# An attention and mixture-of-experts layer: an order worked out by a list scheduler, grouped diagonal tiles, sums of the softmax on other engines

## The chip, the cores and the metric

The kernel runs on one core of a Trainium2 chip. A core has TensorE (PE, matrix products into PSUM), VectorE (DVE), ScalarE (ACT), GpSimd (POOL) and SyncE (SP, which here only issues DMAs), each with an instruction stream of its own; they wait for each other on semaphores. The metric is the device time of the program in microseconds, from first to last instruction. Times are given in us unless marked otherwise.

## The reference

The input is x with 2 sequences of 1024 tokens and 128 features. Two sublayers follow each other, each between two layer normalisations:

```
x = x + layernorm(attention(layernorm(x)))
x = x + layernorm(moe(layernorm(x)))

attention: q = x @ wq                           8 heads of 128
           k, v from a latent of 32 per KV group, 2 groups, 4 heads to a group
           scores = q . k / sqrt(128), causal;  probs = softmax(scores);  y = (probs @ v) @ wo
moe:       32 experts of 64, in 4 groups; the best 2 groups (by the sum of their top 2), then the best 6 experts,
           weights = sigmoid scores of those, normalised, x 0.2
           out = sum of weight * (silu(x @ wg) * (x @ wu)) @ wd  + shared expert + 0.1 * anchor expert (of 16)
```

All products are wanted in about float32 precision. The kernel splits each float32 operand into a rounded high part and the low rest (`_hi`, `_lo`) and adds up three products, hi*hi, lo*hi and hi*lo (the helper `three`).

## The kernel before

**Tiling.** Tokens go in 4 chunks of 512 (two for each sequence). A block n is a chunk and a KV group: 8 blocks of 512 queries times 4 heads. A block of a sequence's first chunk has 4 key tiles of 128, one of the second chunk has 8. The latent of 32 is held three times over (96 rows: hi, hi, lo), so that one matmul of 96 rows gives a score in split precision.

**Two passes.** In the first pass (`p1`, L1046 with mask L1049) scores lie with queries on partitions: DVE takes the row maximum (L782), and ACT takes the exponential with a running sum for the softmax's denominator (L652; each sum is read by an extra accumulator read). The negative maximum, in three parts, becomes three more rows of q: POOL issues three DMAs for them (L587). In the second pass (`p2`, L1077 with mask L1079) scores lie with keys on partitions, ACT writes probabilities (L665), two heads at a time, and PE multiplies them with v (`pv`, L1095) into the bank `acc`.

**Mixture of experts.** An expert tile holds two experts; a chunk has 21 steps (16 expert tiles, 4 anchor tiles, 1 shared), 84 in all. A routed step has 10 matmuls of 512 columns: three for the gate (L974 to L976), three for the up product (the same lines), one that spreads the tokens' weights of this tile's experts over the partitions (L1138), three for the down product (L1150 to L1152). ACT does silu (L676) and the high part of h (L683), DVE two multiplications (L941, L942), POOL the low part (L620).

**Order.** `make_timeline` writes one list of events by hand rules (slots, lags, paces), and every engine walks through that list in order. One PSUM bank `misc` serves every small product, one `acc`, six serve scores. The queries of a block reach their place in 12 pieces by DMAs that SP issues (L521), from `q_hi` and `q_lo`. Weights of the attention are transposed on the chip at the start (L983, L987) and folded into each other (L993, L997).

Of the kernel before, what the change touches and what calls it, by code (L numbers as in the profile page):

```python
# [25 lines left out]
KROWS = QROWS + 3  # L50
# [8 lines left out]
MT = ET + LT + 1  # L59
WROWS = 3 * E + L  # L60
# [8 lines left out]
SBANKS = 6  # L69
KTBUF = 3  # L70
EXP_LAG = 0
DOWN_LAG = 3
AHEAD = 6
TAKE_LAG = 2
TOKEN_PACE = 4
TAIL = 8
SHORT = (1, 5)
SHORT_TAIL = 6
PROJ_LEFT = 4
PV_LAG = 2  # L80
PV_STEP = 3
YL_LAG = 1
QRING = 3


WSPLITS = range(0, MT, 3)
SPLIT_AT = (2, 3, 5)
MISC_KINDS = ("xT", "kproj", "vproj", "proj", "shift", "rb", "post_out", "post_T", "post_logits", "post_cwT", "fin_T")
ROUTE_STEPS = 9
PACE = 3  # L90
QUIET = ("load", "tables", "scale", "wsplit", "post_add", "fin_add")

TAKEN = ("xT", "kproj", "vproj", "proj", "shift", "rb", "post_T", "post_cwT")

TAKES = {"xn_mom": {"ln"}, "post_out": {"ln", "misc", "post"}, "post_logits": {"misc"}, "fin_T": {"ln", "misc"}, **{kind: {"misc"} for kind in TAKEN}}
GIVES = {"xT": {"ln"}, "post_nrm": {"misc"}, "post_T": {"ln"}, "post_logits": {"misc"}, "fin_nrm": {"misc"}, "fin_add": {"ln"}}


def make_timeline():

    line = []
    slots = 0
    held = set()
    agenda = []
# [12 lines left out]

    def may(ev):
        if ev[0] == "proj" and ("take", "xT", CPB * BLOCKS[ev[1]][0] + BLOCKS[ev[1]][1]) not in line:
            return False  # L120
        return not TAKES.get(ev[0], set()) & held

    def tick(limit=1, tensor=True):

        for c in list(agenda):
            while c[1] and c[0] <= slots and may(c[1][0][1]):
                ev = c[1][0][1]
                loud = ev[0] not in QUIET
                if loud and (limit == 0 or (ev[0] in MISC_KINDS and not tensor)):
# [1059 lines left out]
```

## Time and profile before

| | us |
|---|---|
| median of 3 runs | 528.27 (526.51 to 544.34) |
| span of the profiled execution | 536.1 |
| first matmul of a first pass | at 33.59 |
| last attention work, first of the experts | about 306.6 |
| last matmul of the experts | at 526.06 |

| engine | busy us | share of the span |
|---|---|---|
| PE | 467.0 | 87% |
| DVE | 352.8 | 66% |
| ACT | 306.9 | 57% |
| POOL | 200.7 | 37% |

Of the profiled execution the span is known, not its time by the other clock; it lies 1.5% above the median. PE's ends are modelled, so its busy share overstates its work: the distance from one start to the next is the better price of a matmul. The span has four stretches: a start in which little runs, the attention, the experts, and a tail of some 10 us after the last matmul.

### The profile page before, as it was taken

The numbers are of one execution on the slowest core, as the hardware profiler recorded it, in microseconds if no ns is written. First come the engines' busy times: TensorE is split into PE (matmuls) and PEld (weight loads), VectorE is DVE, ScalarE is ACT, GpSimd is POOL, SyncE is SP. The second block draws the span as 40 slices with busy tenths as digits, with TensorE's granted clock in tenths as the row PEclk, the third lists the DMA queues.
The fourth block names the chain that finished last, engine by engine and source line by source line (L and its number), as shares of the span: only waits on it lengthen the run. The fifth ranks groups of instructions, "written<-read, shape, count | busy, mean of one in ns | idle before, by whom it ended". The sixth has DMA issues, their size and how long they took to land.

```text
span 536.1 us, 7733 instructions
## 1 busy us (share of the span) xinstructions
PE 467.0 (87%) x2611; PEld 307.0 (57%) x2611; DVE 352.8 (66%) x937; ACT 306.9 (57%) x687; POOL 200.7 (37%) x216
## 2 busy tenths in 40 slices
PE   3657769889888999889989999999899989989992
PEld 2545445546455545446455667676677656667771
DVE  3345837575666479685692376989776698957662
ACT  2034758747786688898883456454345634445541
POOL 5000226051346001048011155455666456446553
PEclk9999999566996579999995899999999999999997
DMA  6263110300350500201000000000000000000000
GB/s 166 57 140 84 36 26 1 90 3 2 88 106 12 150 1 2 60 4 41 21 4 2 2 0 0 2 0 1 21 1 1 1 1 20 1 0 21 1 1 20
DMA packets 20472, 15.95 MB, mean 30 GB/s; under 512 B 8016, under 2 KB 15856, under 8 KB 20432
## 3 DMA queue, kind: packets, MB, share of 16 engines
q1 hardware_dynamic: 19664, 15.25, 11.6%
q8 instruction: 21, 0.34, 0.3%
q0 software_dynamic: 768, 0.20, 0.2%
q14 instruction: 19, 0.16, 0.1%
HBM read 6.32 MB, written 1.05 MB: 14 GB/s over the span
## 4 chain that ended last, share of the span: by engine, by line
PE 50%; DVE 26%; SPq 6%; POOL 5%; issue 5%; ACT 4%; DMA 1%; POOLq 0%; DVEq 0%; ACTq 0%
PE ps L1077 8%; PE acc L1095 7%; PE ps L1046 6%; DVE nmax_h L782 5%; PE ps L974 4%; DVE act_u L941 4%; SPq L521 4%; PE ps L976 4%; PE ps L975 4%; DVE h_sb L942 3%; ACT ps L652 2%; DVE normed L724 2%; POOL rstd L547 2%; PE acc L1150 2%; DVE stats L703 2%
## 5 line engine op out<-in xcount | busy, mean ns | idle before, releaser
L782 DVE TENSOR_REDUCE nmax_h<-ps 128x1 f32<-128x512 f32 (+3 forms) x192 | 98.0, 550 | 74.4 <-PE ps L1046 52.0
L652 ACT ACTIVATE ps<-ps,nmax_h 128x512 f32<-128x512 f32 (+3 forms) x192 | 106.1, 554 | 56.1 <-DVE nmax_h L782 55.5
L620 POOL TENSOR_TENSOR h_lo<-h_sb,h_hi 128x512 fp32r<-128x512 f32 (+1 forms) x84 | 108.7, 1298 | 78.4 <-ACT h_hi L683 78.4
L676 ACT ACTIVATE act_u<-ps 128x512 f32<-128x512 f32 (+1 forms) x84 | 50.2, 598 | 76.6 <-PE ps L976 76.4
L665 ACT ACTIVATE probs<-ps 128x1024 f32<-128x1024 f32 (+3 forms) x96 | 77.3, 815 | 19.8 <-PE ps L1079 12.5
L1077 PE MATMUL ps<-qst,kst 99*128 99x512 f32 (+3 forms) x192 | 80.5, 488 | 8.7 <-ACT ps L652 7.6
L1046 PE MATMUL ps<-kst,qst 96*128 96x512 f32 (+3 forms) x192 | 77.3, 486 | 10.7 <-DMA qst<-q_lo 9.8
L941 DVE TENSOR_TENSOR act_u<-act_u,ps 128x512 f32<-128x512 f32 x80 | 54.7, 684 | 43.7 <-PE ps L1138 25.8
L974 PE MATMUL ps<-xT_hi,w_hi 128*128 128x512 f32 x168 | 69.1, 412 | 8.4 <-DVE h_sb L942 7.3
L683 ACT ACTIVATE h_hi<-h_sb 128x512 fp32r<-128x512 f32 (+1 forms) x84 | 52.6, 626 | 30.8 <-DVE h_sb L942 29.5
L587 POOL DMA_DIRECT2D qst<-shift_rows x24 | 13.2, 553 | 140.8 <-DVE shift_rows L808 140.8
L976 PE MATMUL ps<-xT_hi,w_lo 128*128 128x512 f32 x168 | 65.6, 391 | 0.0
L975 PE MATMUL ps<-xT_lo,w_hi 128*128 128x512 f32 x168 | 65.6, 390 | 0.0
L1095 PE MATMUL acc<-probs,v_sb 128*32 128x256 f32 (+3 forms) x768 | 58.3, 386 | 3.5 <-ACT probs L665 2.0
L1077 PEld LDWEIGHTS ps<-qst,kst 99*128 99x128 f32 x192 | 43.0, 239 | 31.5 <-ACT ps L652 14.0
L1046 PEld LDWEIGHTS ps<-kst,qst 96*128 96x128 f32 x192 | 42.8, 251 | 30.3 <-DMA qst<-q_lo 10.2
L942 DVE TENSOR_TENSOR h_sb<-act_u,ps 128x512 f32<-128x512 f32 x80 | 55.0, 687 | 2.8
L1150 PE MATMUL acc<-h_hi,wd_hi 128*128 128x512 f32 (+1 forms) x84 | 47.9, 570 | 0.8 <-POOL h_lo L620 0.8
L974 PEld LDWEIGHTS ps<-xT_hi,w_hi 128*128 128x128 f32 x168 | 31.6, 188 | 23.2 <-DVE h_sb L942 16.2
L546 POOL TENSOR_SCALAR var_eps<-mv 128x4 f32<-128x4 f32 x16 | 3.7, 232 | 99.8 <-DVE mv L706 99.8
L652 ACT ACTIVATION_READ_ACCUMULATOR ps<-ps,nmax_h 128x1 f32 x192 | 38.6, 201 | 0.0
L976 PEld LDWEIGHTS ps<-xT_hi,w_lo 128*128 128x128 f32 x168 | 31.5, 188 | 6.9
(163 smaller groups left out, 715.0 us busy)
## 6 DMA issues: line engine op xcount, KB each, us to landing
qst<-q_hi SPq DMA_DIRECT2D x64, 64.0 KB, 2.0
qst<-q_lo SPq DMA_DIRECT2D x32, 64.0 KB, 2.0
x_sb<-in_attn_x SPq DMA_DIRECT2D x4, 256.0 KB, 5.7
kst<-k_hi SPq DMA_DIRECT2D x16, 64.0 KB, 2.0
result<-x_sb SPq DMA_DIRECT2D x4, 256.0 KB, 2.3
raw<-in_attn_wq SPq DMA_DIRECT2D x1, 512.0 KB, 3.8
raw<-in_attn_wo SPq DMA_DIRECT2D x1, 512.0 KB, 5.1
kst<-k_lo SPq DMA_DIRECT2D x8, 64.0 KB, 2.0
```

What stands on the lines that cost most here:

```text
L620: nc.gpsimd.tensor_tensor(h_lo[0:rows, k % 3, :], h_sb[0:rows, k % 2, :], h_hi[0:rows, k % 3, :].bitcast(F32), ALU.subtract).then_inc(h_lo ...
L652: nc.scalar.activation(scores, scores, ACT.Exp, bias=nmax_h[:, n % 2, i, j, h:h + 1], accum_out=sums_h[:, n % 2, i, j, h:h + 1]).then_inc( ...
L665: nc.scalar.activation(probs[:, k % KTBUF, 2 * p:2 * p + 2, off:CH], ps[:, BANK[ev]:BANK[ev] + 2, 0:CH - off], ACT.Exp).then_inc(slot_free, 1)
L782: nc.vector.tensor_reduce(nmax_h[:, n % 2, i, j, h:h + 1], ps[:, BANK[ev], 0:keys_of(ev)], AX.X, ALU.max, negate=True).then_inc(nmax_ready, 1)
L941: link(nc.vector.tensor_tensor(silu_u, silu_u, ps[:, bank + 1, :], ALU.mult))
L942: nc.vector.tensor_tensor(h_sb[:, k % 2, :], silu_u, ps[:, bank + 2, :], ALU.mult).then_inc(h_ready, 1)
L974: nc.tensor.matmul(dst, lhs[0], rhs[0], start=True, stop=False)
L975: nc.tensor.matmul(dst, lhs[0], rhs[1], start=False, stop=False)
L976: return nc.tensor.matmul(dst, lhs[1], rhs[0], start=False, stop=True)
L1046: last = nc.tensor.matmul(ps[:, BANK[ev], 0:keys], qst[0:QROWS, n % QRING, j, P * i:P * i + P], kst[0:QROWS, g, at:at + keys], start=True, ...
L1077: last = nc.tensor.matmul(ps[:, BANK[ev] + r, 0:CH - off], kst[0:KROWS, g, at:at + P], qst[0:KROWS, n % QRING, j, off:CH], start=True, sto ...
L1095: last = nc.tensor.matmul(acc[LAT * j:LAT * j + LAT, cols], v_sb[:, (T // P) * b + kt, LAT * g:LAT * g + LAT], probs[:, k % KTBUF, j, cols ...
```

## The change

Nearly every part of the program is written anew; what is computed stays the same.

- **Order.** `plan` gives every step an engine, a cost, a rank, the steps that it comes after and how many PSUM banks it takes until when; `Order.settle` places at each turn the step that can start first, the smaller rank where several can. Each engine walks its own list. All six banks serve scores, small products and experts alike; two more hold `acc` and `total`.
- **Start.** Small weights come from the host transposed and in one array; the folding (L1256, L1264) stays. Block 0's keys and queries go from PSUM straight to their place (`k0`, `q0`). PE runs 14 extra matmuls at the start (`warm`). SP issues 3 pieces per block for q rather than 12, and one for the rows of the maximum, now two rather than three.
- **First pass.** The exponentials on ACT and their sums are gone. The diagonal key tiles of several heads share a bank, so that 152 maxima remain of 192.
- **Second pass.** The four heads of a diagonal tile share a bank; 152 exponentials of at most 512 columns take the place of 96 of up to 1024. `pv` is 4 matmuls of up to 512 columns per key tile rather than 8 of half as many. The softmax's denominator comes from POOL, which adds the probabilities of two key tiles (`add`, 48 instructions), and PE, which multiplies the sums with ones into `total` (`ones`, 24 times 4 matmuls); DVE turns it into a reciprocal by two transposes (`recip`).
- **Normalisations** are applied by ACT rather than DVE.
- **Experts.** The weights of the experts are ordered so that one spread tile `cwb` serves 16 steps, made by two matmuls per chunk; a routed step has 9 matmuls. POOL multiplies silu's result with `cwb` (`mul`), DVE multiplies with the up product in PSUM (`h`) and takes the low part (`lo`). The routing of a chunk is cut into 24 DVE steps, placed among other work.
- **Tail.** The last normalisation runs in two halves of 256 tokens.

```diff
+def p2_steps(n):
+
+    out = []
+    for kt in range(kts(n)):
+        at = first_col(n, kt)
+        if on_diagonal(n, kt):
+            out.append(("p2", n, kt, 0, REP, at, P))
+            at += P
+        if at < CH:
+            w = CH // (CH - at)
+            w = 4 if w == 4 else 2 if w == 2 else 1
+            out += [("p2", n, kt, j, w, at, CH - at) for j in range(0, REP, w)]
+    return out
...
+        while any(ready.values()):
+            best = None
+            for engine, found in ready.items():
+                options = []
+                for ev in found:
+                    _, _, rank, after, width, _ = steps[ev]
+                    at = max([free[engine]] + [end[a] + HOP for a in after if steps[a][0] != engine])
+                    if width:
+                        at = max(at, min(banks_at(width))[0])
+                    options.append((at, rank, ev))
+                if options:
+                    soon = min(o[0] for o in options)
+                    pick = min((o for o in options if o[0] <= soon), key=lambda o: o[1])
+                    if best is None or pick[0] < best[0]:
+                        best = pick
...
+                        step("POOL", ("add", n, kt, half), 2 * (8 + cols * 252 // 1000), rank - 0.1, ("pv", n, kt - 1),
+                             *[e for e in exps if half in halves_of(e)])
+                    step("PE", ("ones", n, kt - 1), 10 + (CH - first_col(n, kt - 1)) * 17 // 100, rank - 0.2, ("add", n, kt, 0), ("add", n, kt, 1),
+                     kt == 1 and n >= 1 and ("recip", n - 1))
...
+            step("POOL", ("mul", k), 130, rank, ("silu", k), *([("cwb_copy", 0, m), ("cwb_copy", 1, m)] if t == 0 else []))
+            step("PE", ("u", k), 68, rank + 0.5, ("g", k), bank=1, until=("lo", k))
+            step("DVE", ("h", k), 69, rank - 1, ("mul", k), ("u", k))
...
                     for r, part in enumerate((q_hi, q_hi, q_lo)):
-                        for j in range(REP):
-                            sp.dma_start(qst[LAT * r:LAT * r + LAT, n % QRING, j, :].bitcast(F32), part[LAT * j:LAT * j + LAT, :].bitcast(F32)).then_inc(q_in[n % QRING], 16)
-                elif kind == "fin_add":
+                        sp.dma_start(qst[LAT * r:LAT * r + LAT, n % QRING, :, :].bitcast(F32), part[:].bitcast(F32)).then_inc(q_in[n % QRING], 16)
+                elif kind == "s_dma":
+                    n = ev[1]
+                    sp.wait_ge(copied, COPIED["shift_copy", n])
+                    if n >= QRING:
...
+                    nc.gpsimd.tensor_tensor(into, into, probs[:, k % KTBUF, js, cols], ALU.add).then_inc(added, 1)
...
-                    nc.gpsimd.tensor_tensor(h_lo[0:rows, k % 3, :], h_sb[0:rows, k % 2, :], h_hi[0:rows, k % 3, :].bitcast(F32), ALU.subtract).then_inc(h_lo_ready, 1)
...
+                    nc.gpsimd.tensor_tensor(silu[:, k % HRING, :], silu[:, k % HRING, :], cwb[:, m % 2, t // ET, :], ALU.mult).then_inc(scaled_ready, 1)
...
-                    nc.scalar.activation(scores, scores, ACT.Exp, bias=nmax_h[:, n % 2, i, j, h:h + 1],
-                                         accum_out=sums_h[:, n % 2, i, j, h:h + 1]).then_inc(slot_free, 1)
...
+                    link(nc.vector.transpose(rb[:], total[:]))
+                    link(nc.vector.reciprocal(inverse[:], rb[:].rearrange("p (q l) -> p q l", l=LAT)[:, :, 0]))
+                    nc.vector.transpose(rb[:].rearrange("p (q l) -> p q l", l=LAT), inverse[:].unsqueeze(2).to_broadcast([P, CH // LAT, LAT])).then_inc(recip_ready, 1)
...
-                        link(nc.vector.tensor_tensor(silu_u, silu_u, ps[:, bank + 1, :], ALU.mult))
-                        nc.vector.tensor_tensor(h_sb[:, k % 2, :], silu_u, ps[:, bank + 2, :], ALU.mult).then_inc(h_ready, 1)
...
+                    nc.vector.tensor_tensor(up, silu[0:rows, k % HRING, :], up, ALU.mult).then_inc(h_ready, 1)
+                elif kind == "lo":
+                    k = ev[1]
+                    rows = P if k in ROUTED else SI
+                    dve.wait_ge(h_hi_ready, H_HI["hi", k])
...
+                    s = bank(ev)[:, 0:w * cols].rearrange("p (w c) -> p w c", w=w)
+                    last = nc.tensor.matmul(s, kst[0:KROWS, g, at:at + P], qst[0:KROWS, n % QRING, j:j + w, first:first + cols], start=True, stop=not masked)
+                    if masked:
+                        last = nc.tensor.matmul(s, ident_bf[:], mask2[:].unsqueeze(1).to_broadcast([P, w, P]), start=False, stop=True)
...
+                elif kind == "ones":
+                    _, n, kt = ev
+                    cols = slice(first_col(n, kt), CH)
+                    pe.wait_ge(added, max(ADD["add", n, kt + 1, part] for part in range(2)))
+                    if kt == 0 and n >= 1:
+                        pe.wait_ge(recip_ready, n)
+                    for j in range(REP):
+                        last = nc.tensor.matmul(total[LAT * j:LAT * j + LAT, cols], ones[:], probs[:, KT[n, kt] % KTBUF, j, cols],
+                                                start=(kt == 0), stop=(kt == kts(n) - 2))
...
+                    nc.tensor.matmul(bank(ev), sel[:, part, :], cwT[:], start=True, stop=True).then_inc(misc_full, 1)
...
-                    if t < MT - 1:
-                        last = nc.tensor.matmul(ps[:, bank + 2, :], sel[:, t, :], cwT[:, m, :], start=True, stop=True)
```

The first place is PE's list in the experts, two steps of the steady state. Before, a step is three times three matmuls and the spreading matmul L1138:

```order
L974 MATMUL ps<-xT_hi,w_hi 128x512
L975 MATMUL ps<-xT_lo,w_hi 128x512
L976 MATMUL ps<-xT_hi,w_lo 128x512
L974 MATMUL ps<-xT_hi,w_hi 128x512
L975 MATMUL ps<-xT_lo,w_hi 128x512
L976 MATMUL ps<-xT_hi,w_lo 128x512
L1138 MATMUL ps<-cwT,sel 128x512
L1150 MATMUL acc<-h_hi,wd_hi 128x512
L1151 MATMUL acc<-h_lo,wd_hi 128x512
L1152 MATMUL acc<-h_hi,wd_lo 128x512
```

In the changed kernel it is:

```order
L1227 MATMUL ps<-xT_hi,w_hi 128x512
L1228 MATMUL ps<-xT_lo,w_hi 128x512
L1229 MATMUL ps<-xT_hi,w_lo 128x512
L1227 MATMUL ps<-xT_hi,w_hi 128x512
L1228 MATMUL ps<-xT_lo,w_hi 128x512
L1229 MATMUL ps<-xT_hi,w_lo 128x512
L1423 MATMUL acc<-h_hi,wd_hi 128x512
L1424 MATMUL acc<-h_lo,wd_hi 128x512
L1425 MATMUL acc<-h_hi,wd_lo 128x512
```

One matmul of ten has left the step; gate, up and down follow each other as before.

The second place is ACT's list in the middle of the attention. Before, exponentials of the first pass (L652, each followed by its accumulator read) stand between those of the second (L665):

```order
L652 ACTIVATE ps,sums_h<-ps,nmax_h 128x128 x2
L656 ACTIVATE scales<-scales 128x32
L665 ACTIVATE probs<-ps 128x2x384
L665 ACTIVATE probs<-ps 128x2x256
L627 ACTIVATE q_hi<-misc 128x512
L652 ACTIVATE ps,sums_h<-ps,nmax_h 128x256 x2
L665 ACTIVATE probs<-ps 128x2x256
L665 ACTIVATE probs<-ps 128x2x128
```

In the changed kernel ACT has exponentials of the second pass (L885), small copies, and four instructions for each normalisation of a chunk (L838):

```order
L885 ACTIVATE probs<-ps 128x512 x4
L838 ACTIVATE normed_p<-ps,offset,rstd 128x128 x4
L885 ACTIVATE probs<-ps 128x512 x6
L885 ACTIVATE probs<-ps 128x4x128
L885 ACTIVATE probs<-ps 128x384 x4
L885 ACTIVATE probs<-ps 128x4x128
L885 ACTIVATE probs<-ps 128x2x256
L838 ACTIVATE normed_p<-x_sb,offset,rstd 128x128 x4
L872 ACTIVATE shift_rows<-ps 8x512
```

The first pass has left ACT, and the normalisations have come to it.

The third place is POOL's list in the same part of the changed kernel (before, POOL has here the splitting of weights, the shift rows' DMAs and one addition per chunk). L747 is the addition of two key tiles' probabilities, L773 to L779 the splitting of weights, L710 to L713 the scale of a normalisation:

```order
L747 TENSOR_TENSOR probs<-probs 128x2x128 x2
L773 CAST w_hi<-raw 128x384
L774 TENSOR_TENSOR w_lo<-raw,w_hi 128x384
L773 CAST w_hi<-raw 128x256
L774 TENSOR_TENSOR w_lo<-raw,w_hi 128x256
L747 TENSOR_TENSOR probs<-probs 128x1024
L710 TENSOR_SCALAR neg_mean<-mv 128x4
L711 TENSOR_SCALAR var_eps<-mv 128x4
L712 TENSOR_TENSOR rstd<-var_eps,half_power 128x4
L713 TENSOR_TENSOR offset<-neg_mean,rstd 128x4
```

A normalisation's scale and a PE `ones` product now stand behind an addition of two tiles on the same engine.

## Rows read from the trace of the kernel before

**Rows 1.** Busy time by stretch: start:end, length, busy us of each engine (instructions), granted clock, DMA.
```profile
0.00:33.60 33.60, 16.26 (x73) 13.09 (x73) 11.90 (x38) 4.69 (x6) 8.30 (x18) 1.00 0.44 115
...
82.60:195.30 112.70, 101.80 (x612) 59.97 (x608) 71.69 (x183) 81.38 (x210) 35.56 (x49) 0.73 0.22 54
195.30:280.60 85.30, 78.81 (x666) 44.80 (x662) 63.93 (x229) 73.84 (x185) 20.86 (x31) 1.00 0.09 21
...
306.60:527.00 220.40, 207.66 (x924) 148.82 (x916) 165.77 (x371) 107.62 (x181) 122.45 (x101) 1.00 0.02 4
```

**Rows 2.** Chain of waits up to 35 us: start, us, what; a piece that SP issues is SPq.
```profile
5.40 1.04 POOL rstd L547
...
22.29 0.51 SPq L521
...
29.18 0.59 SPq L521
```

**Rows 3.** Timeline of PE around the first matmul of a first pass: start, us, engine, line, tiles.
```profile
33.16 0.63 PE L976 MATMUL misc<-xT_hi,wkv_lo 128*128 128x512 f32 x1
33.59 0.31 PE L1046 MATMUL ps<-kst,qst 96*128 96x128 f32 x1
```

**Rows 4.** Groups of instructions, 195.3 to 280.6, by form: busy us, mean ns | idle before, releaser.
```profile
L1077 PE MATMUL ps<-qst,kst 99*128 99x512 f32 x50 | 18.9, 455 | 2.8 <-ACT ps L652 2.5
L1046 PE MATMUL ps<-kst,qst 96*128 96x512 f32 x32 | 13.5, 468 | 0.6 <-ACT probs L665 0.6
L1095 PE MATMUL acc<-probs,v_sb 128*32 128x256 f32 x204 | 16.6, 395 | 1.2 <-ACT probs L665 0.9 <-issue 0.2
```

**Rows 5.** Timeline of PE at 255, the clock granted in full.
```profile
254.90 0.73 PE L1077 MATMUL ps<-qst,kst 99*128 99x512 f32 x2
255.57 0.64 PE L1095 MATMUL acc<-probs,v_sb 128*32 128x256 f32 x8
256.14 0.73 PE L1077 MATMUL ps<-qst,kst 99*128 99x512 f32 x2
```

**Rows 6.** Groups of instructions over the whole span, as in rows 4.
```profile
L652 ACT ACTIVATE ps<-ps,nmax_h 128x512 f32<-128x512 f32 (+3 forms) x192 | 106.1, 554 | 56.1 <-DVE nmax_h L782 55.5
L652 ACT ACTIVATION_READ_ACCUMULATOR ps<-ps,nmax_h 128x1 f32 x192 | 38.6, 201 | 0.0
L782 DVE TENSOR_REDUCE nmax_h<-ps 128x1 f32<-128x512 f32 (+3 forms) x192 | 98.0, 550 | 74.4 <-PE ps L1046 52.0 <-PE ps L1049 21.7
```

**Rows 7.** ACT's exponentials of the second pass, widest and narrowest form.
```profile
L665 ACT ACTIVATE probs<-ps 128x1024 f32<-128x1024 f32 x48 | 48.9, 1029 | 7.1 <-PE ps L1079 3.8 <-PE ps L1077 3.1
...
L665 ACT ACTIVATE probs<-ps 128x256 f32<-128x256 f32 x16 | 6.1, 384 | 4.8 <-PE ps L1079 3.0 <-PE acc L1095 1.7
```

**Rows 8.** The same as rows 6 over the whole span, the lines of an expert step, and a normalisation.
```profile
L941 DVE TENSOR_TENSOR act_u<-act_u,ps 128x512 f32<-128x512 f32 x80 | 54.7, 684 | 43.7 <-PE ps L1138 25.8 <-POOL h_lo L620 10.1 <-ACT act_u L676 7.3
...
L620 POOL TENSOR_TENSOR h_lo<-h_sb,h_hi 128x512 fp32r<-128x512 f32 x80 | 103.6, 1299 | 72.8 <-ACT h_hi L683 72.8
L676 ACT ACTIVATE act_u<-ps 128x512 f32<-128x512 f32 (+1 forms) x84 | 50.2, 598 | 76.6 <-PE ps L976 76.4
L724 DVE TENSOR_SCALAR normed<-x_sb,mv,rstd 128x128 f32<-128x128 f32 x32 | 11.0, 405 | 4.3 <-POOL rstd L547 4.3
```

**Rows 9.** Timeline of PE in the experts at 483, one step from L1138 to L1138.
```profile
483.03 0.39 PE L1138 MATMUL ps<-cwT,sel 112*128 112x512 bf16 x1
...
485.32 0.39 PE L1138 MATMUL ps<-cwT,sel 112*128 112x512 bf16 x1
```

**Rows 10.** DVE's L876 (both inputs in SBUF): 195.3 to 280.6, then 306.6 to 527.
```profile
L876 DVE TENSOR_TENSOR ties<-ties,lower 128x64 f32<-128x64 f32 x1 | 0.2, 224 | 0.0
...
L876 DVE TENSOR_TENSOR ties<-ties,lower 128x64 f32<-128x64 f32 x2 | 2.5, 1271 | 0.1
```

**Rows 11.** Timeline from the last matmul, all engines: start, us, engine, line [idle before].
```profile
526.06 0.39 PE L1152 MATMUL acc<-h_hi,wd_lo 64*128 64x512 f32 x1
...
533.41 0.37 SPq L525 DMA_DIRECT2D result<-x_sb  x1
```

More of the change, by code:

```diff
@@ new lines, with kts, first_col, pack @@
+ROUTE_STEPS = len(ROUTE_COST)
+ROUTED = {k: n for n, k in enumerate(k for k in range(NU) if k % MT != SHARED)}
+def kts(n):
+    return TPC * (BLOCKS[n][1] + 1)
+def first_col(n, kt):
+    return P * max(0, kt - TPC * BLOCKS[n][1])
+def pack(cols):
+    return 4 if cols == P else 2 if cols == 2 * P else 1
+def p1_steps(n):
+    c = BLOCKS[n][1]
+    out = []
+    for i in range(TPC) if n else reversed(range(TPC)):
+        own = pack(P * (i + 1))
+        out += [("p1", n, i, j, 0, 1) for j in range(REP) if c]
+        out += [("p1", n, i, j, c, own) for j in range(0, REP, own)]
+    return out
@@ new lines, with count @@
+KT_AT = [(n, kt) for n in range(NB) for kt in range(kts(n))]
+KT = {at: k for k, at in enumerate(KT_AT)}
+PLACED, PLAN = plan()
+BANK, BEFORE = PLACED.bank, PLACED.before
+def count(engine, *kinds):
+    return {ev: k + 1 for k, ev in enumerate(e for e in PLAN[engine] if e[0] in kinds)}
+MISC = count("PE", "xT", "k0", "q0", "kproj", "vproj", "proj", "am", "am2", "shift", "post_out", "post_T", "post_logits", "post_cwT", "cwb", "fin_T")
+SCORES = count("PE", "p1", "p2")
+PV = count("PE", "pv")
+ONES = count("PE", "ones")
@@ new lines @@
+G = count("PE", "g")
+U = count("PE", "u")
+DOWN = count("PE", "down")
+HI = count("ACT", "xT_hi", "a3_hi", "a_hi", "k0_hi", "q0_hi", "k_hi", "q_hi", "post_T_hi")
+NORMED = count("ACT", "xn_nrm", "post_nrm", "post_nrm2", "fin_nrm")
+COPIED = count("ACT", "m_copy", "v_copy", "shift_copy", "cwT_copy", "cwb_copy", "post_tanh", "fin_copy")
+EXP = count("ACT", "exp")
+SILU = count("ACT", "silu")
+H_HI = count("ACT", "hi")
+LO = count("DVE", "xT_lo", "a3_lo", "a_lo", "k0_lo", "q0_lo", "k_lo", "q_lo", "post_T_lo")
@@ new lines @@
+MAX = count("DVE", "max")
+MOM = count("DVE", "xn_mom", "post_mom", "post_mom2", "fin_mom")
+H = count("DVE", "h")
+H_LO = count("DVE", "lo")
+RSTD = count("POOL", "xn_rstd", "post_rstd", "post_rstd2", "fin_rstd")
+ADD = count("POOL", "add")
+MUL = count("POOL", "mul")
+WSPLIT = count("POOL", "wsplit")
+LN = {ev: k for k, ev in enumerate(MOM)}
+MOM_OF = {"xn_rstd": "xn_mom", "post_rstd": "post_mom", "post_rstd2": "post_mom2", "fin_rstd": "fin_mom",
+          "xn_nrm": "xn_mom", "post_nrm": "post_mom", "post_nrm2": "post_mom2", "fin_nrm": "fin_mom"}
@@ new lines, in _ @@
+                    for kc in range(CPB * b, CPB * b + c + 1):
+                        if kc:
+                            pe.wait_ge(k_in[kc], 16 * 3)
+                        else:
+                            pe.wait_ge(lo_ready, LO["k0_lo", g])
+                    pe.wait_ge(masks, 3)
+                    bank_turn(ev)
+                    at = T * b + CH * h
+                    keys = p1_cols(ev)
+                    s = bank(ev)[:, 0:w * keys].rearrange("p (w k) -> p w k", w=w)
+                    for r in range(w):
+                        last = nc.tensor.matmul(s[:, r, :], qst[0:QROWS, n % QRING, j + r, P * i:P * i + P], kst[0:QROWS, g, at:at + keys],
+                                                start=(r == 0), stop=(h < c))
```

1700 lines of the change are left out of this document (953 added, 747 removed).

## The prediction, on record before the changed kernel ran

> **What bounds the kernel now.** I read the table of stretches first [rows 1]. Up to 33.6 us PE is busy less than half the time and no score has been computed. From 82.6 to 306.6 lies most of the attention, with a mean granted clock of 0.73 up to 195.3: PE runs at 1.2 GHz for more than half of that stretch. From there to 280.6 it is 1.00, which is 2.4 GHz. From 306.6 to 527 lie the experts, at 1.00 throughout. PE looks busy nearly everywhere, but its ends are modelled, so I price a matmul by the distance between starts.
>
> In the full-clock stretch of the attention (85.3 us) I count what PE did [rows 4, 5]. Two score matmuls of 512 columns take 255.57 - 254.90 = 0.67 us, eight rows of `pv` of 256 columns 0.57 us. So 82 score matmuls of 512 are 27.5 us and 204 rows of `pv` 14.5 us; with the narrower ones and the small products, which I estimate at 26 us, 68 of 85.3 us, or 0.80, were work. What holds PE back is ACT, busy for 73.84 of 85.3 us (0.87) [rows 1]. It does the exponential of both passes, and 201 ns of accumulator reading for each of 192 in the first; DVE's maxima in turn wait 52.0 us for PE, and ACT 55.5 us for them [rows 6].
>
> In the experts a step takes 485.32 - 483.03 = 2.29 us for ten matmuls, 0.229 each [rows 9]. Eighty such steps and four shared ones of nine matmuls are 183 + 8 = 191 us of 220.4.
>
> **The start.** SP's twelve pieces of q take 22.29 to 29.77 (12 rows of about 0.6) [rows 2], and the first score follows at 33.59 [rows 3]. The change writes block 0's q and k straight to their place, and PE no longer transposes the small weights. What is left is a chain: scale of the normalisation to 6.44 [rows 2], then by estimate 0.8 to apply it, 0.7 to transpose, 1.3 for the two halves, 1.3 for three matmuls at half clock (0.43 each, as from 33.16 to 33.59 [rows 3]), 1.3 again for halves; the folded weights a3, which need wq, may end later. That is 12 at the least and 22 if the weights' chain sets the end. I take 15.5: 18 us less. `warm` runs while PE has nothing else, at no cost, unless it goes on past the first transposes, which is inside these bounds.
>
> **Attention.** *ACT* loses the first pass, 106.1 + 38.6 us [rows 6]. The second pass is 152 instructions rather than 96 over the same 73,728 columns: 1024 columns take 1029 ns and 256 take 384 [rows 7], so 0.84 ns per column and 0.17 us beside them, 62 + 26 = 88 us. With normalisations (some ten in the attention, four pieces each of about 0.4 us, as DVE's 405 ns [rows 8]) and copies ACT has some 125 us, and no longer bounds anything.
>
> *PE*, at full clock. A score matmul of 512 costs 0.229 in a run of its kind [rows 9] and 0.335 where kinds alternate [rows 5]; I take 0.28. First pass: 96 of these and 96 narrower ones at 0.2 to 0.33 with their masks (estimates in proportion), 52 us. Second pass: 152 groups at about 0.29, 45 us. `pv`: 24 key tiles of 512 columns at 1.0 (twice 0.57 less a start [rows 5]) and 24 narrower at 0.25 to 0.8, 37 us. New `ones`: 16 at 1.0 and 8 at 0.57, 20 us. Projections, transposes and small products 27 us, and 10 us more for changes of kind: 191 us. Before, the same count without `ones` and with dearer `pv` gives about the same, so PE gains nothing in work; it gains that nobody holds it up.
>
> *DVE* keeps 152 maxima of 97 us in place of 98.0, for the same columns [rows 6], loses the normalisations (11.0 us for those out of SBUF [rows 8], about as much for those out of PSUM) and gains 8 `recip` (three instructions, two of them of 512 columns, each some 0.69 [rows 8]: 13 us). With the low parts, moments and two chunks' routing it has 165 us.
>
> *POOL* gets 48 additions of 32,768 columns in all. By L620, 1299 ns for 512 columns [rows 8], that is 83 us; with what it has there already, 35.6 + 20.9 us [rows 1], about 140 us. A `ones` product waits for an addition, and a probability buffer comes free with it (four buffers): with a pair of full key tiles POOL needs 5.2 us, PE in the second pass alone 5.4 us.
>
> *SP* issues three q pieces per block rather than twelve, and the maximum's rows in one DMA, which POOL issued in three. On SP that one stands behind up to six pieces of 0.6 us [rows 2] and the loads of weights, 2 to 4 us; the first pass of the next block covers it, and where that is used up PE waits so long, once per block, 8 times at the worst (inside the end of 0.80 below).
>
> So the fullest engine after PE has 165 of some 230 us. The old kernel reached 0.80 with ACT at 0.87. I take 0.87 for PE, with ends 0.80 and 0.95: 191 / 0.87 = 220 us (201 to 239). To that I add 10 us for 1.2 GHz: in the first 20 us of the attention PE still waits for tokens and weights. Attention ends at 15.5 + 220 + 10 = 245 us, before at 306.6.
>
> **Experts.** Nine matmuls at 0.229 make a step of 2.06 us: 80 steps 165 us, four shared ones 5.5 (two products, six matmuls), transposes and logits of the chunks some 10: 180 us. DVE has two instructions of 0.684 us in a step, 1.37 as before, POOL 1.30 as before, ACT two instructions of some 0.6 [rows 8]. The spreading matmul, for which DVE waited 25.8 us [rows 8], is gone from the step; what stands in its place is POOL's multiplication between silu and `h`, 1.3 us longer in latency, covered by three buffers rather than two. Before, 29 us of 220.4 were lost, mostly where routing held DVE; routing is now cut into 24 pieces. I take 16 us lost: 196 (188 to 215).
>
> **Tail.** From the last matmul at 526.06 to the store's issue at 533.41 are 7.35 us [rows 11]; in halves the middle steps are half as long and lie beside each other: 4.3, 3 us less.
>
> **Sum.** 536.1 - 18 (start) - 43.6 (306.6 - 33.6 = 273 of attention becomes 229.5) - 24.4 (experts) - 3 = 447 us. The profiled execution lies 1.5% above the median of 528.27, so 447 x 528.27 / 536.1 = 441 us.
>
> **Where a rule speaks against it.** The row: L876, with both inputs in SBUF, took 224 ns where POOL was mostly idle and 1271 ns in the experts, where POOL runs 1299 ns instructions [rows 8, 10]; L941, with one input in PSUM, took 684 ns beside the same POOL. The Trainium skill says in "SBUF — State Buffer", section "Who interferes with whom", that a DVE instruction with two SBUF inputs and a GpSimd instruction lock each other out of a shared port for a whole instruction. The trace agrees, with 1271 against 224 ns. By that rule alone the longer additions would make the second rival below likelier.
>
> **The rivals.**
>
> *(a) PE alone bounds (0.15).* No wait matters and the clock stays up after the start: 15 + 201 + 3 + 190 and 10 behind, 419 on the span and 413. For: no other engine has over 0.72 of the attention. Against: lists fixed in advance by costs that don't meet the chip's durations leave waits on four engines.
>
> *(b) POOL and DVE lock each other out (0.17).* DVE has some 100 instructions in the attention with SBUF inputs alone (rows of maxima, reciprocals, two routings). Where POOL is busy 0.6 of the time with instructions of 1.3 to 2.6 us, each may wait up to 1 to 2.6 us: 40 to 90 us on DVE's 165, which makes DVE the bound, at 205 to 255 of 230, and some 15 us more in the experts. Then the attention takes 20 to 25 us more and the time is 475 to 485. It decides once DVE's stretch passes some 50 us.
>
> *(c) Slower: the clock stays at 1.2 GHz (0.03).* For: 0.43 us per matmul at 33.2 [rows 3] after a start in which PE was half idle, and a mean of 0.73 from 82.6 to 195.3, where waits for ACT and DVE also left it unevenly fed [rows 1, 6]. If the new waits keep PE at 1.2 GHz through the attention, its 191 us become 382: 15 + 382 / 0.95 + 196 + 10 = 623, slower than before. It decides once some 90 us of the attention's full-clock work run at the half clock beyond what I count, which alone costs as much again and brings 447 to 536 on the span. Against: the experts stay at 1.00 with 29 us lost.
>
> *(d) The lists don't fit (0.04).* The changed list keeps engines waiting for each other as much as the old one (0.80 and worse), the experts gain only the tenth matmul: 15.5 + 250 + 205 + 7, 478 on the span and 471.
>
> **The numbers.** The forecast, 441, has 0.61, with its own range of 420 to 465. With (a) below it and (b), (d) above, 405 to 484 holds 8 in 10. A change of 2% is 10.6 us, about what a measurement can tell: 518 and 539 are far from all cases but (c). Faster 0.95, same 0.02, slower 0.03.
>
> **What would show it.** The first score near 15 us; ACT under 0.6 busy in the attention; the attention's end near 245; steps of 2.06 us between the down products; DVE's reciprocal and routing rows at a multiple of their 200 ns would speak for (b), a granted clock of 0.5 beyond 40 us for (c). I am wrong in the main step if PE's starts lie no denser in the attention than 0.80 of its work.

## The result: 438.65 us, the forecast 441, by two misses that nearly cancel

The changed kernel takes 438.65 us (median of 4 runs, 436.96 to 440.96). The ratio to the kernel before is 0.8337, with a 95% interval of 0.8276 to 0.8397. That is inside the range, and close to the 441 us that was forecast. A second measurement beside later runs gave 438.91 (436.47 to 442.81, 6 runs).

The kernel before takes 522 to 551 us, longer where less clock was granted (a mean of 0.94 at 522 us, 0.87 at 551): the ratio is from its shorter, undisturbed runs (spans of 520 to 527 us), while its trace is of a longer one (536.1), so that some 10 of the 98.5 us between the two traces are that run's. Below, a part of the kernel is compared by its stretch in a trace. I cut the span at events that both kernels have: the first score, the first gate product of the experts, the last down product.

| | before | changed | forecast |
|---|---|---|---|
| start, to the first score | 33.6 | 16.9 | 15.5 |
| attention, to the first gate product | 273.2 | 213.8 | 229.5 |
| experts, to the last down product | 219.2 | 199.4 | 195 |
| tail | 10.1 | 7.5 | 7 |
| span | 536.1 | 437.6 | 447 |

The forecast's 196 us for the experts were counted from 306.6 to 527, 1.2 us more than this cut; hence 195.

### The profile after

The first score, the answer to [rows 3], and the tail, the answer to [rows 11], from the timelines of PE and of SP:

```profile
16.93 0.40 PE L1317 MATMUL ps<-kst,qst 96*128 96x512 f32 x1
...
430.10 0.38 PE L1425 MATMUL acc<-h_hi,wd_lo 64*128 64x512 f32 x1
```
```profile
434.35 1.39 SPq L672 DMA_DIRECT2D result<-x_sb  x2
```

The first half's store is issued 4.25 us after the last matmul, where it was 7.35 for the whole. The stretches of the changed kernel, one answer to [rows 1], with columns as there:

```profile
0.00:16.90 16.90, 13.85 (x66) 12.06 (x67) 10.75 (x36) 6.12 (x12) 8.82 (x30) 0.90 0.45 132
16.90:230.70 213.80, 197.29 (x1250) 105.55 (x1248) 157.92 (x388) 108.66 (x219) 121.29 (x121) 0.94 0.28 52
230.70:430.50 199.80, 190.01 (x842) 146.56 (x838) 155.46 (x363) 113.04 (x209) 121.30 (x111) 0.99 0.02 5
430.50:437.60 7.10, 1.11 (x4) 0.71 (x4) 3.05 (x16) 1.91 (x6) 1.49 (x2) 0.51 0.12 37
```

For the attention of the kernel before, the two stretches that [rows 1] did not show in this cut:

```profile
33.60:82.60 49.00, 36.84 (x146) 24.46 (x144) 28.57 (x76) 28.89 (x92) 8.14 (x10) 1.00 0.28 61
82.60:306.80 224.20, 205.80 (x1490) 120.31 (x1486) 144.12 (x442) 165.58 (x409) 59.23 (x85) 0.82 0.15 35
```

The 1.00 of the first of these is not a grant but the lack of a record. The distances of its masked scores, at 45, 60, 74 and 81 us, are those of 1.2 GHz; at 45 us 0.67 us from one score to the next:

```profile
45.06 0.78 PE L1046 MATMUL ps<-kst,qst 96*128 96x512 f32 x1
45.64 0.33 PE L1049 MATMUL ps<-mask,ident_bf 128*128 128x128 bf16 x1
45.73 0.78 PE L1046 MATMUL ps<-kst,qst 96*128 96x512 f32 x1
```

The same pair in the changed kernel, at 2.4 GHz, takes 0.36 us:

```profile
17.88 0.48 PE L1317 MATMUL ps<-kst,qst 96*128 96x512 f32 x1
18.20 0.23 PE L1320 MATMUL ps<-mask,ident_bf 128*128 128x128 bf16 x1
18.24 0.48 PE L1317 MATMUL ps<-kst,qst 96*128 96x512 f32 x1
```

From these rows the gain of the attention can be taken apart. Before, PE was busy for 36.84 + 205.80 = 242.6 us, and ran at 1.2 GHz for the first 49.0 us and 78.5 of recorded grants (a mean of 0.82 over 224.2 us is as much, within its rounding), 127.5 us in all. Changed, it is busy for 197.3 us, with 27.3 us at 1.2 GHz. PE's busy time within those stretches is the number behind the length; before, from 82.6 us on:

```profile
96.30:116.80 20.50, 19.35 (x96) 12.19 (x92) 12.31 (x36) 11.86 (x32) 3.96 (x7) 0.50 0.21 51
120.20:130.40 10.20, 9.71 (x51) 6.60 (x52) 4.66 (x10) 7.77 (x25) 3.01 (x5) 0.50 0.01 2
164.60:195.30 30.70, 30.70 (x151) 16.81 (x149) 16.10 (x48) 21.58 (x53) 5.25 (x7) 0.50 0.27 70
280.60:297.70 17.10, 17.10 (x102) 9.40 (x99) 5.22 (x17) 7.09 (x11) 1.54 (x3) 0.50 0.01 2
```

and changed:

```profile
27.90:34.70 6.80, 4.89 (x17) 4.10 (x18) 3.27 (x8) 1.76 (x5) 2.28 (x4) 0.50 0.52 189
58.60:65.40 6.80, 6.75 (x25) 3.58 (x25) 4.76 (x10) 1.77 (x5) 4.39 (x6) 0.50 0.83 119
120.10:130.30 10.20, 9.30 (x24) 4.36 (x24) 7.30 (x13) 4.67 (x8) 2.35 (x4) 0.50 0.00 0
222.50:225.90 3.40, 3.40 (x15) 2.13 (x15) 3.23 (x23) 1.12 (x3) 0.00 (x0) 0.50 0.00 0
```

So PE was busy at 1.2 GHz for 36.8 + 76.9 = 113.7 us before and for 24.3 now. Of that time 0.46 is lost by the pair of scores above (0.67 us for 0.36), or half by the ratio of the clocks (1.2 to 2.4 GHz): 53 to 57 us before, 11 to 12 now. By this estimate **41 to 45 of the 59.4 us came with the clock**. PE's idle time fell from 30.6 to 16.5 us, 14 us more. What is left, 186 to 190 us of full-clock work before and 185 to 186 now, is nearly the same: the sums by `ones` cost about what the longer products of `pv` save. The 191 us of the forecast were 3% too many.

The busy share of PE hardly shows any of this (0.89 before, 0.92 now), and in two of the old stretches at 1.2 GHz PE was busy throughout. In which part the 10 us named above fall, no trace tells. The one other trace of the same attention code (the kernel before without the spreading matmul, below) has an attention of 274.5 us with 129.6 at 1.2 GHz, a second one of the changed kernel 212.6 with 23.9.

The costliest waits of PE in the changed kernel (us in all, times, the longest):

```profile
PE ps L1317 <- DMA qst<-q_lo: 6.1, 2, 3.8
PE ps L1388 <- DVE weights L1140: 4.6, 2, 3.1
PE acc L1423 <- DVE h_lo L1159: 4.0, 6, 1.2
PE ps L1372 <- ACT silu L913: 3.2, 1, 3.2
PE total L1362 <- POOL probs L747: 3.2, 3, 1.8
```

L1423 and one of the two L1388 (1.5 us) lie among the experts' steps, L1372 at the passage to them, the others before it. The step is what was priced: in this piece of timeline, from a first product to that of the next step, nine matmuls take 382.69 - 380.62 = 2.07 us, against 2.29 for ten in [rows 9].

```profile
380.62 0.39 PE L1227 MATMUL ps<-xT_hi,w_hi 128*128 128x512 f32 x1
...
382.00 0.40 PE L1423 MATMUL acc<-h_hi,wd_hi 128*128 128x512 f32 x1
382.24 0.39 PE L1424 MATMUL acc<-h_lo,wd_hi 128*128 128x512 f32 x1
382.46 0.40 PE L1425 MATMUL acc<-h_hi,wd_lo 128*128 128x512 f32 x1
382.69 0.39 PE L1227 MATMUL ps<-xT_hi,w_hi 128*128 128x512 f32 x1
```

### The profile page after: what moved, and what is told of

Its sections match the earlier page's. It is cut to its first block, busy times and chain, and to the rows that moved or that the text cites. A ratio compares the mean times of both kernels' runs of the same rounds, so it can differ in the third digit from the quotient of the medians.

```text
span 437.6 us, 6989 instructions
## 1 busy us (share of the span) xinstructions
PE 402.3 (92%) x2156; PEld 264.9 (61%) x2156; DVE 327.2 (75%) x800; ACT 229.7 (53%) x445; POOL 252.9 (58%) x263
## 3 DMA queue, kind: packets, MB, share of 16 engines
q1 hardware_dynamic: 9584, 13.49, 15.5%
## 4 chain that ended last, share of the span: by engine, by line
PE 65%; DVE 21%; issue 4%; DMA 3%; ACT 3%; POOL 2%; SPq 1%; POOLq 0%; DVEq 0%; ACTq 0%
PE ps L1317 8%; PE ps L1338 8%; PE ps L1227 7%; PE ps L1229 7%; PE ps L1228 7%; PE acc L1352 7%; PE acc L1423 4%; DMA qst<-q_lo 3%; PE total L1362 3%; PE acc L1425 3%; PE acc L1424 3%; DVE ps L1154 3%; DVE nmax_h L1039 2%; PE ps L1372 2%; DVE h_lo L1159 2%
## 5 line engine op out<-in xcount | busy, mean ns | idle before, releaser
L787 POOL TENSOR_TENSOR silu<-silu,cwb 128x512 f32<-128x512 f32 x80 | 103.2, 1296 | 64.0 <-ACT silu L913 63.2
L885 ACT ACTIVATE probs<-ps 128x512 f32<-128x512 f32 (+1 forms) x152 | 80.1, 578 | 72.6 <-PE ps L1338 38.1
L747 POOL TENSOR_TENSOR probs<-probs 128x768 f32<-128x768 f32 (+2 forms) x48 | 78.1, 1645 | 59.9 <-ACT probs L885 37.1
L1159 DVE TENSOR_TENSOR h_lo<-ps,h_hi 128x512 fp32r<-128x512 f32 (+1 forms) x84 | 57.2, 685 | 22.0 <-ACT h_hi L923 21.5
L1154 DVE TENSOR_TENSOR ps<-silu,ps 128x512 f32<-128x512 f32 (+1 forms) x84 | 57.8, 691 | 16.1 <-POOL silu L787 12.9
L923 ACT ACTIVATE h_hi<-ps 128x512 fp32r<-128x512 f32 (+1 forms) x84 | 50.1, 598 | 32.4 <-DVE ps L1154 28.0
L913 ACT ACTIVATE silu<-ps 128x512 f32<-128x512 f32 x80 | 47.6, 599 | 36.4 <-PE ps L1229 30.9
L1338 PE MATMUL ps<-qst,kst 98*128 98x512 f32 (+1 forms) x152 | 64.1, 462 | 1.5 <-ACT probs L885 0.5
L1317 PEld LDWEIGHTS ps<-kst,qst 96*128 96x128 f32 x192 | 36.3, 204 | 30.7 <-issue 20.5
L1352 PE MATMUL acc<-probs,v_sb 128*32 128x512 f32 (+3 forms) x384 | 41.2, 513 | 0.3 <-issue 0.2
L1338 PEld LDWEIGHTS ps<-qst,kst 98*128 98x128 f32 x152 | 29.8, 204 | 16.5 <-issue 14.9
L1423 PE MATMUL acc<-h_hi,wd_hi 128*128 128x512 f32 (+1 forms) x84 | 35.5, 423 | 4.2 <-DVE h_lo L1159 4.0
L1424 PE MATMUL acc<-h_lo,wd_hi 128*128 128x512 f32 (+1 forms) x84 | 33.2, 395 | 0.0
```

What stands on the lines that cost most here:

```text
L747: nc.gpsimd.tensor_tensor(into, into, probs[:, k % KTBUF, js, cols], ALU.add).then_inc(added, 1)
L787: nc.gpsimd.tensor_tensor(silu[:, k % HRING, :], silu[:, k % HRING, :], cwb[:, m % 2, t // ET, :], ALU.mult).then_inc(scaled_ready, 1)
L885: nc.scalar.activation(probs[:, k % KTBUF, j:j + w, at:at + cols], bank(full)[:, 0:w * cols].rearrange("p (w c) -> p w c", w=w), ACT.Exp). ...
L1154: nc.vector.tensor_tensor(up, silu[0:rows, k % HRING, :], up, ALU.mult).then_inc(h_ready, 1)
L1159: nc.vector.tensor_tensor(h_lo[0:rows, k % HRING, :], bank(("u", k))[0:rows], h_hi[0:rows, k % HRING, :].bitcast(F32), ALU.subtract).then_ ...
L1317: last = nc.tensor.matmul(s[:, r, :], qst[0:QROWS, n % QRING, j + r, P * i:P * i + P], kst[0:QROWS, g, at:at + keys], start=(r == 0), stop ...
```

## Experiments

Two theories of the attention were tried against each other, that ACT held it and that the new order, with or without the clock, made the gain; then what sets the experts' pace, what the additions on POOL cost, and two small edits that the waits above point to.

### The first-pass exponential put back

```diff
+            step("ACT", once, wide * (42 + cols * 80 // 1000), rank, peak, x and ("once", *steps[x - 1][1:]))
...
-                        pe.wait_ge(max_ready, MAX["max", *user[1:]])
+                        pe.wait_ge(once_done, ONCE["once", *user[1:]])
...
+                        last = nc.scalar.activation(scores, scores, ACT.Exp, bias=nmax_h[:, n % 2, i, j + r, h:h + 1],
+                                                    accum_out=sums_h[:, n % 2, i, j + r, h:h + 1])
```

> The changed kernel with one part undone: ACT again takes the exponential of the first pass, with its running sum and accumulator read (192 instructions in the plan, each first-pass bank is held until it is done; the sums are not used further). Theory A, ACT held the attention before and its relief is what shortened it: ACT gets some 145 us more (192 of about 0.55 and 0.2) on the 116 it has between 17 and 246, 261 us of busy time in a stretch of 229.5, so the attention must grow to 275 to 300 us and the time from 438.65 to 485 to 510, with ACT at 0.85 to 0.95 busy there. Rival B, the new order and PE's longer products shortened it and ACT does not matter: under 450.

492.67 us (490.51 to 496.54): 54 us more, as theory A had it. The lists are worked out anew with these steps in them. The attention's stretch, and the two groups that came back:

```profile
14.80:281.50 266.70, 219.68 (x1249) 109.88 (x1247) 153.28 (x365) 212.77 (x607) 121.65 (x124) 0.88 0.23 42
```
```profile
L885 ACT ACTIVATE ps<-ps,nmax_h 128x512 f32<-128x512 f32 (+3 forms) x192 | 108.9, 573 | 35.5 <-DVE nmax_h L1056 34.9
...
L885 ACT ACTIVATION_READ_ACCUMULATOR ps<-ps,nmax_h 128x1 f32 x192 | 43.4, 226 | 0.0
```

It takes 266.7 us, near the 273.2 of before, with 64.9 us at 1.2 GHz and 47 us of idle PE. ACT is busy for 0.80 of it. On the expectation's own cut, to the last out product (14.75 to 296.4), the attention is 281.7 us, inside its 275 to 300, with ACT at 0.78 and not 0.85 to 0.95. So with the new order and everything else in place, this one part is worth most of the gain of the attention.

### The same part taken out of the kernel before

```diff
-                    nc.scalar.activation(scores, scores, ACT.Exp, bias=nmax_h[:, n % 2, i, j, h:h + 1],
-                                         accum_out=sums_h[:, n % 2, i, j, h:h + 1]).then_inc(slot_free, 1)
+                    nc.scalar.activation(sums_h[:, n % 2, i, j, h:h + 1], scores[:, 0:1], ACT.Exp, bias=nmax_h[:, n % 2, i, j, h:h + 1]).then_inc(slot_free, 1)
```

> The kernel before, its order untouched, with ACT's first-pass exponential cut to one column and without the running sum (so the softmax's denominators are left out of the computation). ACT loses some 100 us (192 times about 0.33, and the accumulator reads 38.6) of 232 in the attention. Theory A, ACT held PE at 0.80 there: the attention shortens by 35 to 50 us, ratio 0.91 to 0.935. Rival B, the old order's hand rules, the waits for DMAs and the 1.2 GHz stretches held it: under 10 us, ratio over 0.98.

523.98 us (510.45 to 541.15), the kernel before beside it 528.55 (527.21 to 545.41). Theory A falls for the old kernel: in the trace its attention still takes 261.8 us, 11 less, and lowest run against lowest is 16.8 us. That is more than rival B's 10 and half of theory A's least.

```profile
33.50:295.30 261.80, 236.49 (x1632) 140.89 (x1630) 172.52 (x518) 129.00 (x308) 67.54 (x94) 0.86 0.18 41
```

ACT's busy time in the attention fell from 194.5 (not the 232 of the expectation) to 129 us, but PE's busy time from 242.6 only to 236.5. The time at 1.2 GHz hardly moved: 71.7 us of recorded grants from 78.5. ACT waited for DVE's maxima instead, 98.5 us in place of the 55.5 of [rows 6]:

```profile
ACT sums_h L652 <- DVE nmax_h L781: 98.5, 121, 6.4
```

### And the maxima thinned as well

```diff
-                    nc.vector.tensor_reduce(nmax_h[:, n % 2, i, j, h:h + 1], ps[:, BANK[ev], 0:keys_of(ev)],
+                    nc.vector.tensor_reduce(nmax_h[:, n % 2, i, j, h:h + 1], ps[:, BANK[ev], 0:64],
```

> The kernel before with the first-pass exponential of one column (as in the run before it) and the maxima taken over 64 columns rather than up to 512, so that neither ACT nor DVE can hold the first pass (the softmax is left out of the reference's form: maxima and denominators are of a part). Relieving ACT alone took the attention from 273 to 262 us only. Theory C, DVE's maxima were next in line behind ACT: the attention falls to 210 to 235 us. Rival D, the order and the 1.2 GHz stretches that come with it (49 us from 33.6 to 82.6, and 72 after that) hold PE: it stays at 245 us or more, with 90 us or more at 1.2 GHz.

491.47 us (489.09 to 493.68), the kernel before beside it 537.24 (522.87 to 548.0); lowest against lowest is 33.8 us, and by the traces the attention is 47.9 us shorter.

```profile
33.40:258.70 225.30, 207.80 (x1632) 128.21 (x1630) 113.88 (x518) 126.02 (x308) 66.93 (x94) 0.94 0.21 48
```

Theory C holds. The old order can do the attention in 225.3 us, if neither DVE nor ACT holds a first-pass bank long. So the order alone was not the limit: in the kernel before a bank went from PE to DVE's maximum, from there to ACT's exponential, and only then back. PE had the same matmuls in that run; it was at 1.2 GHz for 27.3 us of recorded grants, in place of 78.5 (and in the first 30 us of the attention, of which there is no record, in place of 49).

The changed kernel reaches 213.8 us with the maxima at full width (DVE busy for 157.9 us of them and all else). So it takes both: ACT's step gone from the first pass, and lists in which PE does not wait for DVE's maxima though they are as long as before. Which rule of the list does the second (banks for all purposes, their release by the maximum, or the packing of 192 maxima into 152) was not taken apart and stays open.

### A tenth matmul in the experts' step

```diff
+                    if k in ROUTED:
+                        nc.tensor.matmul(total[:], sel[:, t // ET, :], spread[:], start=True, stop=True)
```

> The changed kernel with a tenth matmul of 512 columns in each of the 80 routed expert steps (a product of the selection matrix with a constant, into the bank of the sums, which nothing reads). Theory A, PE's matmuls alone set the experts' pace now: 80 x 0.229 = 18.3 us more, 457. Rival B, waits between the engines or DVE set it: less than 5 us more, under 444.

457.61 us (454.15 to 460.08), 19 us more, 457 expected by theory A. The experts' stretch grew by 17.5 us, from 199.8 to 217.3:

```profile
227.80:445.10 217.30, 206.17 (x922) 150.65 (x918) 157.51 (x363) 113.30 (x210) 120.93 (x111) 0.99 0.02 4
```

The tenth matmul is paid nearly in full (18.3 us by its price): the experts are bound by PE.

### The tenth matmul taken out of the kernel before

```diff
-                    if t < MT - 1:
+                    if k < 2:
                         last = nc.tensor.matmul(ps[:, bank + 2, :], sel[:, t, :], cwT[:, m, :], start=True, stop=True)
```

> The kernel before with the spreading matmul only in the first two expert steps (the later steps multiply with what stands in the bank, so the weights of the experts are left out of the computation). Theory A, PE's ten matmuls set the step also before: 78 x 0.229 = 18 us less, ratio 0.966. Rival B, DVE's second multiplication and POOL's low part set it (DVE waited 25.8 us for this matmul, but PE also waited 7.3 us for DVE): under 6 us less, ratio over 0.99.

530.9 us (518.6 to 531.75) against 528.55, which the scatter doesn't tell apart; lowest against lowest is 8.6 us. By the traces the experts went from 219.2 to 210.7 us, 8.5 and not 18, so both theories are half right. PE's wait for DVE's multiplications grew as the matmul went, from 7.3 us in 14 waits to

```profile
PE ps L974 <- DVE h_sb L942: 15.9, 20, 2.3
```

In the old kernel half of the matmul's price lay on the path; without it PE came sooner to a wait for the two multiplications that stand in series on DVE. In the changed kernel a tenth matmul is paid nearly in full, and between gate and down product the same work is spread over POOL, DVE and ACT; that the spreading makes the difference was not tried by itself.

### No additions on POOL

```diff
-                if kt % 2:
-                    for half in range(2):
-                        step("POOL", ("add", n, kt, half), 2 * (8 + cols * 252 // 1000), rank - 0.1, ("pv", n, kt - 1),
-                             *[e for e in exps if half in halves_of(e)])
...
+                step("PE", ("ones", n, kt), 10 + cols * 17 // 100, rank - 0.2, *exps, kt == 0 and n >= 1 and ("recip", n - 1))
```

> The changed kernel without POOL's additions: PE multiplies every key tile with ones, not every second one. POOL loses 78 us; PE gains 8 products of 512 columns at 0.97, 8 of 384 at about 0.78 and 8 of 128 at about 0.36, 17 us. Theory A, PE bounds the attention: 12 to 17 us slower, 450 to 456. Rival B, POOL's long instructions on the port that DVE shares with it (or POOL itself) hold the attention: no slower, 430 to 440; in both the rows of DVE with SBUF inputs alone return to their short times.

441.21 us (440.39 to 442.5), 2.6 us more, between the theories. By the expectation PE has 17 us more to do, and the attention grows by 5.3 us only:

```profile
14.80:233.90 219.10, 206.19 (x1458) 111.08 (x1456) 143.24 (x355) 109.75 (x223) 47.98 (x79) 0.95 0.27 51
```

The rest is seen: PE is idle for 12.9 us in place of 16.5, and at 1.2 GHz for 20.5 in place of 27.3 (busy for 15.7 of them in place of 24.3, some 4 us less lost), together 8 us; and the full-clock work, counted as above, grew by 13 us, not 17. The start and the experts are 2 us shorter each. Rows of DVE with inputs in SBUF alone are short again, as both theories said. In the changed kernel, and then without the additions, the routing of the chunk that falls into the attention:

```profile
L1132 DVE TENSOR_SCALAR wsum<-wsum 128x4 f32<-128x4 f32 x1 | 1.7, 1699 | 0.0
L1128 DVE TENSOR_SCALAR dist<-dist 128x64 f32<-128x64 f32 x1 | 1.5, 1512 | 0.0
```
```profile
L1120 DVE TENSOR_SCALAR dist<-dist 128x64 f32<-128x64 f32 x1 | 0.2, 184 | 0.0
L1124 DVE TENSOR_SCALAR wsum<-wsum 128x4 f32<-128x4 f32 x1 | 0.2, 171 | 0.0
```

The Trainium skill's rule on the port that DVE and GpSimd share ("SBUF — State Buffer", section "Who interferes with whom"), which counts `tensor_scalar` among the operations that can contend for it, agrees with this, 1512 ns against 184. But what the stretched rows take beyond their short times comes to some 12 us of DVE's time in the attention, not 40 to 90, and DVE had room for it.

### The start without its extra matmuls

```diff
-WARM = 14
+WARM = 0
...
-    step("PE", ("warm",), 560, 0)
+    step("PE", ("warm",), 0, 0)
```

> The changed kernel without the 14 matmuls at the start. Theory A: they fill time in which PE has nothing to do, and PE's clock is granted in full earlier for them; without them the matmuls from 7.5 to 17 us run longer at 1.2 GHz and the first score comes 1 to 3 us later: 440 to 442. Rival B: they only delay the first weight products, which start at 7.55 right behind them: the first score comes up to 2 us sooner, 436 to 438.

439.3 us (438.93 to 439.46), no difference to be told from 438.65. In the trace the first score came at 19.0, later than in all nine traces that have the extra matmuls (14.8 to 18.2). The 16 weight products behind them show why; with the extra matmuls, and then without:

```profile
7.55 1.87 PE L1256 MATMUL ps<-small_w,raw 128*128 128x32 f32 x16
```
```profile
7.02 3.60 PE L1256 MATMUL ps<-small_w,raw 128*128 128x32 f32 x16 [7.02 <-DMA raw<-in_attn_wq]
```

Without them these products start only 0.5 us sooner, when a weight has landed, and take 3.60 us, where they take 1.87 to 1.94 in the nine traces. So theory A's mechanism, an earlier full clock, is there, and rival B's delay is 0.5 us; but the whole time lies between the two forecasts and does not tell them apart, as the first score moves by 3 us from trace to trace anyway.

### Two edits that PE's waits point to

```diff
                     for r, part in enumerate((q_hi, q_hi, q_lo)):
+                        if r == 2:
+                            sp.wait_ge(lo_ready, LO["q_lo", n])
```

> The changed kernel with the two high pieces of q issued as soon as the high part is there, not behind the low part. PE waits twice, 6.1 us in all, for the last piece, and the clock falls after it (27.9 to 34.7). Theory A, issue and landing of three pieces in a row cause that wait: 1 to 4 us less, 435 to 438. Rival B, the last piece lands when it does because the tokens' and weights' loads share the engines: no change.

436.15 us (434.06 to 440.69). It was run again, with the changed kernel itself beside it:

> The changed kernel itself, as the measure for the two runs beside it: 438.7 within 0.5%.

> The changed kernel with the high pieces of q issued before the low part is there, against the changed kernel on the same chip. Theory A, a first score 2 us sooner in its trace was the clock's doing at the start (the same code up to there), and the pieces give 0 to 2 us: 436.5 to 438.7. Rival B, they give the 2.5 us that the first comparison showed, or more: under 436.5.

435.84 us (433.37 to 439.93) against 438.91: 0.7% less, the same side as the first time. PE's wait for the last piece fell from 6.1 us (5.4 in the trace beside it) to

```profile
PE ps L1319 <- DMA qst<-q_lo: 2.7, 1, 2.7
```

and the time at 1.2 GHz in the attention to 17.1 us (23.9 in the trace beside it). Of the difference between these two traces 5.2 us lie in the attention and 1.4 before the first score, where the code is the same. It is the fastest version here. The median falls in rival B's range, but the gain of 3.1 us is small beside the scatter of single runs, which does not exclude theory A's.

```diff
+        if m == 0:
+            rank = 6.5
         step("PE", ("post_cwT", m), 45, rank + pace * ROUTE_STEPS, ("route", m, ROUTE_STEPS - 1), bank=1, until=("cwT_copy", m))
```

> The changed kernel with the transposes of chunk 0's expert weights placed later in PE's list (rank 6.5 rather than 3.6), so that PE does not wait 3.1 us for a DVE whose routing rows POOL stretched. Theory A, that wait and the 10 us at 1.2 GHz right behind it (120.1 to 130.3, some 5 us lost) are the price of the shared port: 4 to 8 us less, 431 to 435. Rival B, the additions' waits before it (1.8 us) bring the clock down by themselves, or it falls elsewhere: under 2 us less.

441.22 us (435.34 to 446.14). The wait for the routing is gone from PE's list of waits, and the clock fell none the less, from 123.0 to 133.3 us. Theory A falls: no time was gained, and the clock falls without that wait too.

> Both together, no additions on POOL and early pieces of q. Theory A, the additions' price (waits of PE for POOL, routing rows stretched on DVE, 10 us more at 1.2 GHz) about equals the 17 us of products with ones that they save: 437 to 441. Rival B, without POOL in the way the earlier pieces bring the clock up sooner: under 435.

439.53 us (437.25 to 442.52), as theory A had it. Beside the early pieces alone (435.84) that is 3.7 us more, as it was 2.6 more without them: the additions save a little more than they cost, some 3 us, which single runs hardly show.

## Why the prediction was right, step by step

- **Start.** Right: 16.9 for 15.5, within 12 to 22. The five traces of the changed kernel and of its two small edits lie between 14.9 and 18.2. How much of the 16.7 us saved came from each part of the start (q and k straight to their place, weights transposed by the host) was not tried.
- **ACT.** Its 125 us in the attention were 109 to the first gate product. That ACT's relief shortens the attention held in the new order (54 us when put back). The step "what holds PE back is ACT" did not hold as it stood: in the old order ACT's relief alone brought 11 us in the trace (17 lowest against lowest), and 48 (34) only together with DVE's maxima. The busy share of 0.87 named the last of two engines in series, not the one limit.
- **PE's share.** The mis-sized term. I took 191 / 0.87 + 10 = 230 us; measured are 185 to 186 us of full-clock work, 16.5 idle, 11 to 12 lost to 1.2 GHz, 214. Work and idle alone make 0.92, between the 0.87 and the end of 0.95. The 10 us for the clock were right on the new side, but the forecast left the clock hidden in the old 273 us, where it cost 53 to 57. So most of the gain had the wrong name: the text said that nobody holds PE up, the rows say that PE has the full clock more of the time. The time at 1.2 GHz follows the first pass both ways: from 27.3 to 64.9 us with ACT's exponential put back, from 127.5 to some 57 with exponential and maxima thinned in the old kernel.
- **The products.** `pv` of a full key tile was put at 1.0; 0.97 is the distance in the changed kernel, from 194.75 to 195.72. The additions took 78 us of POOL's time for 83.
- **Experts.** 199.4 us for 195. The step of 2.07 us and PE-bound experts held. Of the 19 us beyond the 180 of products, 9.5 go at the passage from the attention (230.7 to 246.4, in which only 6.2 us are expert products): the last products of the attention, a wait of 3.2 us for silu (239.7 to 243.1, L1372 above), and 1.2 GHz from 243.0 to 246.4. Waits after it are 5.9 us, and 4 stay open. The routing still has a part: the chain that leads to that wait runs through DVE's routing rows from 226.7 to 236.4, behind which stand a normalisation on DVE and POOL and POOL's first multiplication of silu.
- **Sum.** The span was forecast at 447 and is 437.6. From it I went down by 1.5% to the median, as the profiled execution of the kernel before lay that much above its own. The changed kernel has no such gap: its runs take 2 us more than their spans (439.61 for 437.6) and agree within 1%. So the forecast should have read 449, and the attention's 16 us, against 4.6 too few in the experts and 1.4 at the start, are what the correction to 441 happened to cover.
- **Rivals.** (a) was nearest in its mechanism, PE with little waiting, but PE did not have the full clock. (b): the lock is there, at under a third of its lowest price (12 us for 40 to 90). (c): the opposite of it happened, 27.3 us at 1.2 GHz for 127.5. (d) did not.

## What to carry to other kernels

Where TensorE's clock is not full in a long stretch, price that stretch at full clock first: the busy share (0.89 and 0.92 here) does not show the 53 to 57 us that 1.2 GHz cost, and a change that feeds the engine better may gain them beside the idle time. A wait that one engine ends may be held by two in series; taking one away (11 us by the traces) and both (48 us) shows it, and a change may need the freed bank as much as the freed engine. An undo in the new kernel and the same part alone in the old one can give 54 and 11 to 17 us: neither is "the" worth of a part.

## What the runs showed of the hardware

- The grant of the clock differs from run to run of the same code: the first score of the changed kernel's code came at 14.9 to 18.2 us in the five traces, with the grant falling to 1.2 GHz between 10 and 17 us in four of them and not in the fifth.
- A busy TensorE is not one at full clock: from 164.6 to 195.3 us of the old trace PE was busy for all of 30.7 us, at 1.2 GHz throughout.
- A POOL addition of 128 x 1024 took 2375 ns, less than twice the 1299 ns of 512 columns, and stretched DVE's rows with inputs in SBUF alone up to 1699 ns, where 170 are usual.
